# Cross attention scores as side by side 64-row matmuls of one head each, with a pair of maxima between their halves

## Chip, core and metric

The kernel runs on one core of a Trainium2 chip. The metric is the device time of one execution in microseconds (us), taken as the median of several runs. All times below come from runs of the kernel before and from one profiled execution of it.

## What is computed

Four layers run over a batch of B = 32 sequences of N = 100 tokens with H = 128 features and 16 heads of 8 features each. Three of them (L0, L1 and L3) are transformer layers: self attention, cross attention to a context of S = 1444 keys, and an MLP. L2 is a router layer. The change touches only the cross attention, which the three transformer layers have in this form:

```python
q = (norm(x) @ Wq).reshape(B, N, 16, 8).transpose(0, 2, 1, 3)
k = (ctx @ Wk).reshape(B, S, 16, 8).transpose(0, 2, 1, 3)      # S = 1444
v = (ctx @ Wv).reshape(B, S, 16, 8).transpose(0, 2, 1, 3)
w = softmax(einsum('bhqd,bhkd->bhqk', q, k) * 8 ** -0.5)
x = x + einsum('bhqk,bhkd->bhqd', w, v).reshape(B, N, 128) @ Wo + bo
```

## The kernel before

`cross_attention_phase` is one pipeline over the 32 batches. One pass of its body is called a slot here; slot t does the scores, exponentials and values of batch t, most row maxima of batch t + 1, the first maxima of batch t + 2, and preparation for batches t + 2 and t + 3. Each engine runs its own program in a fixed order, and semaphores tie them together.

The numbers stand as several bf16 parts. A head's keys and queries take 48 rows of a stack (`CROWS`, six products of parts by 8 features) and three more rows for the negated row maximum against rows of ones (`CROWS_NEG` = 51). `g.kst[s]` holds for each of 8 head pairs j the keys of head j in rows 0 to 50 and those of head j + 8 in rows 64 to 114. `g.qst[s]` has the queries: 200 columns per pair, where columns 0 to 99 are filled in the upper 64 rows and columns 100 to 199 in the lower 64, and the rest is zero. That zero fill is three memsets on POOL at the head of each cross phase (L1530), for which the SP queue waits.

A slot goes over 12 key tiles of 128 keys (the last has 36), called kt = 0 to 11. For each, PE (`pe_slot`) issues in this order:

- the scores (L1158, `pe_scores`): two halves of four matmuls, each over all 128 rows with 200 columns, so that one matmul gives the scores of both heads of a pair. Each half fills two PSUM banks, and waits until the exponential of the same half of the key tile before is done;
- a pair of maxima matmuls (L1137, `pe_max`): queries as weights, 482 or 480 keys as moving columns, the two heads of a pair in rows 0 to 47 and 64 to 111, in two PSUM banks;
- the values of the key tile before (L1175, `pe_values`): 32 matmuls with 9 weight columns and 100 moving columns, four side by side in 32-column groups;
- a second pair of maxima matmuls;
- at some key tiles a preparation step (`PREPS`): keys (L1114), values (L1120) or a transposition (L1106) of a coming batch. L0 and L1 have nine of them at five key tiles, L3 has six at six key tiles.

The maxima (48 per slot, called x = 0 to 47, four per key tile) and the preparation steps share a ring of three PSUM banks (`ring_tables`, `pe_ring_free`). A maxima matmul may start when what stood three places before it in the ring has been read: a maximum by DVE (L1294, `dve_max`, one reduction each), a preparation step by ACT. At two places the ring skips a bank. Besides the 48 reductions DVE copies the output of the batch before (L1323, once per slot after x = 2), folds the maxima (L1300) and makes the negated maxima (L1311 to L1318). In L0 it also takes statistics of a coming context (L1269, L1277). ACT does two exponentials per key tile (L1249) and reads the preparation steps. In its program, too, the order is fixed.

The code of the functions that the change touches, and of what calls them:

Of the kernel before, what the change touches and what calls it, by code (L numbers as in the profile page):

```python
# [5 lines left out]
BF16 = mybir.dt.bfloat16  # L6
# [978 lines left out]
def cross_attention_phase(g, wk, kb, wv, context):  # L985
# [16 lines left out]
    CUTS = [(0, S)] if normed else [(0, BANK), (BANK, 2 * BANK), (2 * BANK, S)]  # L1002
    ST_BANK, O_BANK, RING = 0, 4 * BANK, 5 * BANK
    TURN_KT = 8
    QHALF, KROWS = HALF, P
    K_RUNS = ((0, 3), (3, 2), (5, 1))
    KW = 16 * 2 * len(K_RUNS)
    Q_SLOTS = ((0, 3), (3, 2), (5, 1))
# [12 lines left out]
    with ExitStack() as st:  # L1021
# [30 lines left out]
        st_full, exp_done, pv_done = sem("scores_full"), sem("exp_done"), sem("pv_done")  # L1052
        o_read, o_moved = sem("o_read"), slots("o_moved")
        ones, zeros, ctx_std, stacks_set = sem("ones"), sem("zeros"), sem("ctx_std"), sem("stacks_set")
        ones_written, queries_zeroed, ctx_kept = sem("ones_written"), sem("queries_zeroed"), sem("ctx_kept")
        set_up = 1 + 2 * LAG


# [65 lines left out]
        def pe_max(slot, x):  # L1124

            k, t = max_tile(slot, x)
            if k is None:
                return
            s, r = k.s, k.r
            if t == 0:  # L1130
                wait(g.pe, k_loaded[s], 16 * (r + 1))
                wait(g.pe, qst_loaded[s], 16 * 12 * (r + 1))
            pe_ring_free(slot, x)
            at = bank_of(x)
            e, c, j = t % 2, (t // 2) % 3, t // 6
            a, w, row0 = starts[c], widths[c], HALF * e
            nc.tensor.matmul(ps[0:N, at:at + w], g.qst[s][row0:row0 + CROWS, j, N * e:N * e + N], g.kst[s][row0:row0 + CROWS, j, a:a + w],  # L1137
                             start=True, stop=True).then_inc(m_full, 1)

        def pe_turn_max(slot):  # L1140
# [8 lines left out]
        def pe_scores(k, n):  # L1149

            b, s, r = k.b, k.s, k.r
            kt, hf = n // 2, n % 2
            if n == 0:
                wait(g.pe, neg_loaded[s], 16 * 6 * (r + 1))
            wait(g.pe, exp_done, H2 * b + n - 1)
            for jj in range(4):
                o = ST_BANK + (2 * hf + jj // 2) * BANK + 2 * N * (jj % 2)
                ins = nc.tensor.matmul(ps[0:kts[kt], o:o + 2 * N], g.kst[s][0:KROWS, 4 * hf + jj, 128 * kt:128 * kt + kts[kt]],  # L1158
                                       g.qst[s][0:KROWS, 4 * hf + jj, :], start=True, stop=True)
            ins.then_inc(st_full, 1)  # L1160

        def pe_values(k, kt):


            b, s, r = k.b, k.s, k.r
            if kt == 0:
                wait(g.pe, o_read, b)
                wait(g.pe, p_read, S1 * b + PREP_INDEX["V2"] + 1)
            wait(g.pe, exp_done, H2 * b + 2 * kt + 2)
            for hf in range(2):  # L1170
                for e in range(2):
                    for jj in range(4):
                        h, q = 8 * e + 4 * hf + jj, 32 * jj
                        o = O_BANK + N * (2 * e + hf)
                        ins = nc.tensor.matmul(ps[q:q + VW, o:o + N], vals[s][:, kt, h, :],  # L1175
                                               probs[kt % 2][hf][:, N * (2 * jj + e):N * (2 * jj + e) + N],
                                               start=(kt == 0 and hf == 0 and e == 0), stop=(kt == KT - 1),
                                               skip_group_check=True)
            ins.then_inc(pv_done, 1)

        def pe_slot(slot):

            k, before = slot.k(0), slot.k(-1)
            for kt in range(KT):
                if k is not None:
                    pe_scores(k, 2 * kt)
                    pe_scores(k, 2 * kt + 1)
                pe_max(slot, 4 * kt)
                pe_max(slot, 4 * kt + 1)
                if kt == 0 and before is not None:  # L1190
                    pe_values(before, KT - 1)
                if kt and k is not None:
# [206 lines left out]
        def sp_stacks(k):  # L1399
# [7 lines left out]
            for e in range(2):  # L1407
                for part, (first, copies) in enumerate(Q_SLOTS):
                    src = g.qx[b // per, e, part].rearrange("(d j) n -> d j n", j=PAIRS)[:, :, N * (b % per):N * (b % per) + N]
                    for slot in range(first, first + copies):  # L1410
                        at = QHALF * e + HD * slot
                        sp.dma_start(g.qst[s][at:at + HD, :, N * e:N * e + N], src).then_inc(qst_loaded[s], 16)

        def sp_negmax(k):
            b, s, r = k.b, k.s, k.r
# [1 line left out]
            wait(sp, neg_steps, 4 * b + 4)  # L1417
            for e in range(2):
                for part in range(3):
                    at = QHALF * e + CROWS + part  # L1420
                    sp.dma_start(g.qst[s][at:at + 1, :, N * e:N * e + N], nparts[8 * e:8 * e + 8, part, :]).then_inc(neg_loaded[s], 16)

        def sp_keep_ctx(k):
            b, s, sp = k.b, k.s, g.sp
# [44 lines left out]
        with nc.Block() as block:  # L1469
# [56 lines left out]
            @block.gpsimd  # L1526
            def _(pool):
                g.pool = pool
                for s in range(LAG):
                    nc.gpsimd.memset(g.qst[s][:, :, :], 0.0).then_inc(queries_zeroed, 1)  # L1530
                if normed:
                    pool_norm(first)
                for b in range(-3, 1):
# [8 lines left out]
            def _(sp):  # L1542
# [3 lines left out]
                if normed:  # L1546
# [3 lines left out]
                            rows = slice(HALF * e + CROWS, HALF * e + HALF)  # L1550
                            sp.dma_start(g.kscr[s][rows, :], g.kst[0][rows, :, :].rearrange("p j n -> p (j n)")).then_inc(ones_written, 16)
                    sp.wait_ge(ones_written, 16 * 2 * LAG)
                sp.wait_ge(queries_zeroed, LAG)
                for b in range(-3, 1):
                    sp_slot(known(b))
                for i in range(loops):
# [407 lines left out]
def stack_scope(g, stack):  # L1964
# [1 line left out]
    nc = g.nc  # L1966
    g.serial += 1
    g.kst = [stack.enter_context(nc.sbuf_tensor(f"kst{s}_{g.serial}", [P, PAIRS, S], BF16)) for s in range(LAG)]
    g.qst = [stack.enter_context(nc.sbuf_tensor(f"qst{s}_{g.serial}", [P, PAIRS, 2 * N], BF16)) for s in range(LAG)]


def transformer_layer(g, a, pre, names, eps, l1):
# [166 lines left out]
```

## Time and profile before

| | us |
|---|---|
| median of 3 runs | 5788.03 |
| lowest and highest run | 5786.43, 5789.98 |
| span of the profiled execution, first to last instruction | 5784.8 |
| PE busy in it | 4939.3 (85%) |
| DVE busy in it | 3879.1 (67%) |
| ACT busy in it | 2941.4 (51%) |
| POOL busy in it | 1483.5 (26%) |
| maxima on DVE (L1294), busy | 2721.6 |
| scores on PE (L1158), busy | 999.1 |

The profiled execution was taken apart from the timed runs; its span is 3.2 us under their median, which is what lies around the first and the last instruction. In the page a group of instructions stands with its line, engine, result and inputs, shapes, count, then busy time, the mean ns of one, and the idle time of its engine just before them with what ended it. Matmuls are pipelined: the busy time of a run of them holds the tail of the last one, so the time from the start of one run to the start of the next says more of PE than the busy times do.

### The profile page before, as it was taken

To read this page: it belongs to the slowest core of one execution; us is meant where nothing else is said; L and a number is where in the kernel's file an instruction comes from. 1 tells how busy PE (TensorE), PEld (TensorE's weight loads), DVE (VectorE), ACT (ScalarE), POOL (GpSimd) and SP (SyncE) were. 2 spreads that over 40 slices of the span, in tenths; PEclk is the share of its full clock that TensorE was granted. 3 is DMA by queue.
4 is the path that set the end of the run, shared out by engine and by line. 5 is a ranking of instruction groups with operands and counts; after the bars stand their busy time and mean duration, and the time that the engine had idled before them with its cause. 6 is when DMAs were issued, how large, how long until landed. Compare 5 with 4: busy or idle time off the path is not lost. (4 is left out here: it accounts for less than half of the span.)

```text
span 5784.8 us, 149703 instructions
## 1 busy us (share of the span) xinstructions
PE 4939.3 (85%) x63218; PEld 3160.8 (55%) x63218; DVE 3879.1 (67%) x7814; ACT 2941.4 (51%) x4527; POOL 1483.5 (26%) x1198
## 2 busy tenths in 40 slices
PE   4858999999997676999999997888585899999998
PEld 2624555555564453666666663564363466666664
DVE  4537787888873554777777773555553788888883
ACT  2324666666664332666666663215322466666655
POOL 1024343443420104233332310000202333333320
PEclk7667999999998667999999998999766799999998
DMA  3334545545430425655565530540242555555540
GB/s 80 65 82 149 174 148 163 157 154 173 148 112 12 83 50 178 192 187 179 185 193 189 179 117 17 169 159 1 62 70 74 169 179 177 176 177 178 178 137 16
DMA packets 481593, 764.82 MB, mean 132 GB/s; under 512 B 144922, under 2 KB 381883, under 8 KB 468539
## 3 DMA queue, kind: packets, MB, share of 16 engines
q1 hardware_dynamic: 462394, 741.14, 43.1%
q10 hardware_dynamic: 18528, 14.11, 1.1%
q8 instruction: 499, 8.18, 0.6%
q14 instruction: 172, 1.40, 0.1%
HBM read 465.48 MB, written 287.75 MB: 130 GB/s over the span
## 5 line engine op out<-in xcount | busy, mean ns | idle before, releaser
L1294 DVE TENSOR_REDUCE maxima<-ps 100x1 f32<-100x482 f32 (+1 forms) x4608 | 2721.6, 650 | 829.4 <-PE ps L1137 822.6
L1249 ACT ACTIVATE probs<-ps 128x800 f32<-128x800 f32 (+1 forms) x2304 | 1799.8, 835 | 603.2 <-PE ps L1158 601.4
L1137 PE MATMUL ps<-kst,qst 48*100 48x482 bf16 (+1 forms) x4608 | 1101.4, 412 | 101.2 <-DMA qst<-cross_q_parts 49.3
L1346 POOL TENSOR_TENSOR kparts<-kf,zero 128x512 bf16<-128x512 f32 (+2 forms) x448 | 546.6, 1220 | 2103.5 <-ACT kf L1221 2064.2
L1175 PE MATMUL ps<-probs,vals 128*9 128x100 f32 x36864 | 1012.1, 250 | 5.5 <-ACT probs L1249 0.8
L1158 PE MATMUL ps<-qst,kst 128*128 128x200 bf16 (+1 forms) x9216 | 999.1, 250 | 10.3 <-DMA qst<-nparts 4.1
L1158 PEld LDWEIGHTS ps<-qst,kst 128*128 128x128 bf16 (+1 forms) x9216 | 761.4, 98 | 264.1 <-issue 152.8
L1175 PEld LDWEIGHTS ps<-probs,vals 128*9 128x9 f32 x36864 | 734.1, 90 | 255.1 <-issue 225.7
L1137 PEld LDWEIGHTS ps<-kst,qst 48*100 48x100 bf16 x4608 | 335.3, 119 | 616.6 <-DVE maxima L1294 325.9
L1227 ACT ACTIVATE vals<-ps 128x512 f32<-128x512 f32 (+1 forms) x288 | 162.1, 563 | 493.4 <-PE ps L1120 493.4
L1221 ACT ACTIVATE kf<-ps,perm_b_L 128x512 f32<-128x512 f32 (+1 forms) x288 | 190.5, 662 | 351.6 <-PE ps L1114 340.4
L1114 PE MATMUL ps<-ctxT,perm_wk_L 128*128 128x512 f32 (+1 forms) x576 | 305.6, 633 | 61.4 <-DVE maxima L1294 32.9
L763 ACT ACTIVATE probs<-ps 100x800 f32<-100x800 f32 x192 | 159.7, 837 | 366.5 <-PE ps L711 362.6
L1377 POOL TENSOR_TENSOR kparts<-kf,kparts 128x512 bf16<-128x512 f32 (+2 forms) x224 | 306.6, 1369 | 17.6
L1373 POOL TENSOR_TENSOR kf<-kf,kparts 128x512 f32<-128x512 f32 (+2 forms) x224 | 305.4, 1363 | 17.6
L775 DVE TENSOR_REDUCE maxima<-ps 100x4 f32<-100x400 f32 x384 | 205.6, 571 | 142.6 <-PE ps L689 141.8
L1120 PE MATMUL ps<-wkv_L,ctxT 128*128 128x128 f32 (+1 forms) x1536 | 227.8, 293 | 36.6 <-DVE maxima L1294 33.2
L689 PE MATMUL ps<-kst 96*100 96x100 bf16 x1152 | 143.9, 289 | 129.6 <-DMA kst<-k_parts 101.8
L1120 PEld LDWEIGHTS ps<-wkv_L,ctxT 128*128 128x128 f32 (+1 forms) x1536 | 184.3, 190 | 91.7 <-DVE maxima L1294 79.2
L689 PEld LDWEIGHTS ps<-kst 96*100 96x100 bf16 x1152 | 119.6, 193 | 154.8 <-issue 103.7
L1106 PE MATMUL ps<-ident,ctok 128*128 128x128 f32 (+1 forms) x768 | 131.2, 292 | 80.0 <-POOL ctok L1359 42.8
L1114 PEld LDWEIGHTS ps<-ctxT,perm_wk_L 128*128 128x128 f32 x576 | 95.3, 196 | 163.8 <-DVE maxima L1294 110.9
(261 smaller groups left out, 4528.8 us busy)
## 6 DMA issues: line engine op xcount, KB each, us to landing
kst<-ctx_k_stack SPq DMA_DIRECT2D x96, 2888.0 KB
ctx_k_stack<-kparts SPq DMA_DIRECT2D x192, 541.5 KB
ctx_k_stack<-kparts SPq DMA_DIRECT2D x192, 361.0 KB
ctok<-in_ctx_dram SPq DMA_DIRECT2D x64, 704.0 KB
ctx_k_stack<-kparts SPq DMA_DIRECT2D x192, 180.5 KB
ctx_turned<-ctxT SPq DMA_DIRECT2D x32, 722.0 KB, 3.3
cT<-ctx_turned SPq DMA_DIRECT2D x32, 722.0 KB, 5.5
ctxT<-ctx_turned SPq DMA_DIRECT2D x32, 722.0 KB
```

Of the source, the lines that this page charges most:

```text
L689: ins = nc.tensor.matmul(ps[0:N, o:o + N], queries[s][0:SROWS, h // 2, q0:q0 + N], keys[0:SROWS, h // 2, k0:k0 + N], start=True, stop=True)
L775: nc.vector.tensor_reduce(maxima[:, t // 4, c:c + 4], ps[0:N, at:at + CH].rearrange("p (h k) -> p h k", h=4), AX.X, ALU.max).then_inc(m_re ...
L1114: ins = nc.tensor.matmul(ps[:, at:at + w], wk, turned[s][:, a:a + w], start=True, stop=True)
L1120: ins = nc.tensor.matmul(ps[0:n, at + 128 * q:at + 128 * q + 128], turned[s][:, 128 * kt:128 * kt + n], wv, start=True, stop=True)
L1137: nc.tensor.matmul(ps[0:N, at:at + w], g.qst[s][row0:row0 + CROWS, j, N * e:N * e + N], g.kst[s][row0:row0 + CROWS, j, a:a + w], start=Tru ...
L1158: ins = nc.tensor.matmul(ps[0:kts[kt], o:o + 2 * N], g.kst[s][0:KROWS, 4 * hf + jj, 128 * kt:128 * kt + kts[kt]], g.qst[s][0:KROWS, 4 * hf ...
L1175: ins = nc.tensor.matmul(ps[q:q + VW, o:o + N], vals[s][:, kt, h, :], probs[kt % 2][hf][:, N * (2 * jj + e):N * (2 * jj + e) + N], start=( ...
L1249: nc.scalar.activation(probs[kt % 2][hf][0:kts[kt], :].rearrange("p (k n) -> p k n", k=2), src, ACT.Exp).then_inc(exp_done, 1)
L1294: nc.vector.reduce_max(maxima[:, col:col + 1], ps[0:N, at:at + widths[c]], AX.X).then_inc(m_read, 1)
L1346: return nc.gpsimd.tensor_tensor(out, src, g.zero[0:src.shape[0], 0:1].to_broadcast(list(src.shape)), ALU.add)
L1373: nc.gpsimd.tensor_tensor(kf[:, a:z], kf[:, a:z], parts[:, 0, a:z], ALU.subtract).then_inc(split, 1)
L1377: nc.gpsimd.tensor_tensor(parts[:, 2, a:z], kf[:, a:z], parts[:, 1, a:z], ALU.subtract).then_inc(parts_ready, 1)
```

## The change

The scores are cut into twice as many matmuls. Each has one head: 51 rows, at row 0 or at row 64, and 100 columns. The two heads of a pair follow each other and write into different PSUM banks of the half (bank e instead of bank jj // 2), and `pe_values` reads the probabilities in the new places. `g.qst` has 100 columns per pair instead of 200 and holds no zeros, so the memsets on POOL and the SP wait for them go, and the query and negated-maximum DMAs write to rows without a column offset. In `pe_slot` the second half of the scores now stands behind the first pair of maxima.

```diff
-            nc.tensor.matmul(ps[0:N, at:at + w], g.qst[s][row0:row0 + CROWS, j, N * e:N * e + N], g.kst[s][row0:row0 + CROWS, j, a:a + w],
+            nc.tensor.matmul(ps[0:N, at:at + w], g.qst[s][row0:row0 + CROWS, j, :], g.kst[s][row0:row0 + CROWS, j, a:a + w],
...
             for jj in range(4):
-                o = ST_BANK + (2 * hf + jj // 2) * BANK + 2 * N * (jj % 2)
-                ins = nc.tensor.matmul(ps[0:kts[kt], o:o + 2 * N], g.kst[s][0:KROWS, 4 * hf + jj, 128 * kt:128 * kt + kts[kt]],
-                                       g.qst[s][0:KROWS, 4 * hf + jj, :], start=True, stop=True)
+                for e in range(2):
+                    o = ST_BANK + (2 * hf + e) * BANK + N * jj
+                    rows = slice(HALF * e, HALF * e + CROWS_NEG)
+                    ins = nc.tensor.matmul(ps[0:kts[kt], o:o + N], g.kst[s][rows, 4 * hf + jj, 128 * kt:128 * kt + kts[kt]],
+                                           g.qst[s][rows, 4 * hf + jj, :], start=True, stop=True)
             ins.then_inc(st_full, 1)
...
-                                               probs[kt % 2][hf][:, N * (2 * jj + e):N * (2 * jj + e) + N],
+                                               probs[kt % 2][hf][:, N * (4 * e + jj):N * (4 * e + jj) + N],
...
                 if k is not None:
                     pe_scores(k, 2 * kt)
-                    pe_scores(k, 2 * kt + 1)
                 pe_max(slot, 4 * kt)
                 pe_max(slot, 4 * kt + 1)
+                if k is not None:
+                    pe_scores(k, 2 * kt + 1)
...
-                        at = QHALF * e + HD * slot
-                        sp.dma_start(g.qst[s][at:at + HD, :, N * e:N * e + N], src).then_inc(qst_loaded[s], 16)
+                        at = HALF * e + HD * slot
+                        sp.dma_start(g.qst[s][at:at + HD, :, :], src).then_inc(qst_loaded[s], 16)
...
-                for s in range(LAG):
-                    nc.gpsimd.memset(g.qst[s][:, :, :], 0.0).then_inc(queries_zeroed, 1)
...
-                sp.wait_ge(queries_zeroed, LAG)
...
-    g.qst = [stack.enter_context(nc.sbuf_tensor(f"qst{s}_{g.serial}", [P, PAIRS, 2 * N], BF16)) for s in range(LAG)]
+    g.qst = [stack.enter_context(nc.sbuf_tensor(f"qst{s}_{g.serial}", [P, PAIRS, N], BF16)) for s in range(LAG)]
```

PE's order before, in a looped slot of L3, from the end of key tile 5 to the start of key tile 7, with the key preparation L1114 at the end of key tile 6. L1158 is the scores, L1137 the maxima, L1175 the values:

```order
L1137 MATMUL ps<-kst1_419,qst1_419 100x482 x2
L1158 MATMUL ps<-qst0_419,kst0_419 128x200 x8
L1137 MATMUL ps<-kst1_419,qst1_419 100x480 x2
L1175 MATMUL ps<-probs10_509,vals0_509 9x100 x8
L1175 MATMUL ps<-probs11_509,vals0_509 9x100 x8
L1137 MATMUL ps<-kst1_419,qst1_419 100x482 x2
L1114 MATMUL ps<-ctxT0_509,perm_wk_L3 128x512
L1158 MATMUL ps<-qst0_419,kst0_419 128x200 x8
L1137 MATMUL ps<-kst1_419,qst1_419 100x482 x2
```

The same place in the changed kernel, where L1159 is the scores, L1136 the maxima, L1176 the values and L1113 the key preparation:

```order
L1136 MATMUL ps<-kst1_417,qst1_417 100x482 x2
L1159 MATMUL ps<-qst0_417,kst0_417 128x100 x8
L1136 MATMUL ps<-kst1_417,qst1_417 100x480 x2
L1159 MATMUL ps<-qst0_417,kst0_417 128x100 x8
L1176 MATMUL ps<-probs10_507,vals0_507 9x100 x8
L1176 MATMUL ps<-probs11_507,vals0_507 9x100 x8
L1136 MATMUL ps<-kst1_417,qst1_417 100x482 x2
L1113 MATMUL ps<-ctxT0_507,perm_wk_L3 128x512
L1159 MATMUL ps<-qst0_417,kst0_417 128x100 x8
L1136 MATMUL ps<-kst1_417,qst1_417 100x482 x2
```

Between a preparation step, or a second pair of maxima, and the next first pair there now stands half of the scores instead of all; between the first pair and the second there stand the other half and the values, where only the values stood. The program's count x8 holds 8 matmuls of 100 columns for a half, where it held 8 of 200 columns for both halves.

## Rows read from the trace of the kernel before

**Rows 1.** Page: parts 1 and 5 (busy, mean ns, idle before).
```profile
PE 4939.3 (85%) x63218; PEld 3160.8 (55%) x63218; DVE 3879.1 (67%) x7814; ACT 2941.4 (51%) x4527; POOL 1483.5 (26%) x1198
...
L1294 DVE TENSOR_REDUCE maxima<-ps 100x1 f32<-100x482 f32 (+1 forms) x4608 | 2721.6, 650 | 829.4 <-PE ps L1137 822.6
...
L1158 PEld LDWEIGHTS ps<-qst,kst 128*128 128x128 bf16 (+1 forms) x9216 | 761.4, 98 | 264.1 <-issue 152.8
```
**Rows 2.** Windows: L0's prologue, last slot, steady L3: PE, PEld, DVE, ACT, POOL, PEclk.
```profile
470.00:500.00 30.00, 26.18 (x59) 8.41 (x59) 22.48 (x55) 6.26 (x9) 16.77 (x8) 0.50 0.22 57
...
1734.00:1750.00 16.00, 15.73 (x367) 11.25 (x367) 0.00 (x0) 14.50 (x20) 0.00 (x0) 1.00 0.05 12
...
4700.00:5300.00 600.00, 567.48 (x9267) 371.15 (x9265) 491.76 (x899) 363.84 (x514) 212.75 (x204) 1.00 0.56 176
```
**Rows 3.** Timeline of DVE, one slot of L3: start, us, group, idle before.
```profile
5048.99 0.57 DVE L1323 COPY osb<-ps 128x400 f32<-128x400 f32 x1
```
**Rows 4.** The same timeline, further in that slot.
```profile
5050.76 2.37 DVE L1294 TENSOR_REDUCE maxima<-ps 100x1 f32<-100x482 f32 x4 [0.64 <-PE ps L1137]
...
5063.72 4.67 DVE L1294 TENSOR_REDUCE maxima<-ps 100x1 f32<-100x482 f32 x8 [1.10 <-PE ps L1137]
5069.45 2.37 DVE L1294 TENSOR_REDUCE maxima<-ps 100x1 f32<-100x482 f32 x4 [1.07 <-PE ps L1137]
...
5072.77 2.37 DVE L1294 TENSOR_REDUCE maxima<-ps 100x1 f32<-100x482 f32 x4 [0.70 <-PE ps L1137]
...
5076.07 6.92 DVE L1294 TENSOR_REDUCE maxima<-ps 100x1 f32<-100x480 f32 x12
5083.45 1.80 DVE L1294 TENSOR_REDUCE maxima<-ps 100x1 f32<-100x480 f32 x3 [0.45 <-PE ps L1137]
5085.17 0.56 DVE L1323 COPY osb<-ps 128x400 f32<-128x400 f32 x1
```
**Rows 5.** Timeline of PE in that slot, key tiles 6 and 7.
```profile
5066.72 0.41 PE L1137 MATMUL ps<-kst,qst 48*100 48x482 bf16 x2
5067.27 1.13 PE L1114 MATMUL ps<-ctxT,perm_wk_L 128*128 128x512 f32 x2 [0.15 <-DVE maxima L1294]
5068.23 0.85 PE L1158 MATMUL ps<-qst,kst 128*128 128x200 bf16 x8
5069.02 0.41 PE L1137 MATMUL ps<-kst,qst 48*100 48x482 bf16 x2
5069.35 0.88 PE L1175 MATMUL ps<-probs,vals 128*9 128x100 f32 x32
5070.16 0.41 PE L1137 MATMUL ps<-kst,qst 48*100 48x480 bf16 x2
```
**Rows 6.** Timeline of PE at the end of that slot.
```profile
5081.33 0.40 PE L1137 MATMUL ps<-kst,qst 48*100 48x482 bf16 x1
5081.89 0.40 PE L1137 MATMUL ps<-kst,qst 48*100 48x482 bf16 x1 [0.15 <-DVE maxima L1294]
5082.22 0.86 PE L1158 MATMUL ps<-qst,kst 128*128 128x200 bf16 x8
```
**Rows 7.** Timeline of PE in a self attention at the full clock.
```profile
228.77 0.54 PE L689 MATMUL ps<-kst,qextra 96*100 96x100 bf16 x8
```
**Rows 8.** Timeline of DVE in a slot of L1.
```profile
2863.80 2.37 DVE L1294 TENSOR_REDUCE maxima<-ps 100x1 f32<-100x482 f32 x4 [2.03 <-PE ps L1137]
```
**Rows 9.** Timeline of DVE in L0: statistics between maxima, and a slot's start.
```profile
1147.56 0.64 DVE L1294 TENSOR_REDUCE maxima<-ps 100x1 f32<-100x482 f32 x1
...
1148.32 0.64 DVE L1294 TENSOR_REDUCE maxima<-ps 100x1 f32<-100x480 f32 x1
...
1184.39 1.80 DVE L1294 TENSOR_REDUCE maxima<-ps 100x1 f32<-100x480 f32 x3 [0.82 <-PE ps L1137]
```
**Rows 10.** Timeline of POOL at the head of L1's cross phase.
```profile
2182.26 4.17 POOL L1530 MEMSET qst<- 128x1600 bf16 x3 [6.90 <-POOLq L264]
...
2193.32 1.04 POOL L1346 TENSOR_TENSOR kparts<-kf,zero 128x512 bf16<-128x512 f32 x1 [6.88 <-ACT kf L1221]
```

More of the change, by code:

```diff
@@ L1004, in cross_attention_phase @@
     TURN_KT = 8
-    QHALF, KROWS = HALF, P
     K_RUNS = ((0, 3), (3, 2), (5, 1))
@@ L1054, in cross_attention_phase @@
         ones, zeros, ctx_std, stacks_set = sem("ones"), sem("zeros"), sem("ctx_std"), sem("stacks_set")
-        ones_written, queries_zeroed, ctx_kept = sem("ones_written"), sem("queries_zeroed"), sem("ctx_kept")
+        ones_written, ctx_kept = sem("ones_written"), sem("ctx_kept")
         set_up = 1 + 2 * LAG
@@ L1419, in sp_negmax @@
                 for part in range(3):
-                    at = QHALF * e + CROWS + part
-                    sp.dma_start(g.qst[s][at:at + 1, :, N * e:N * e + N], nparts[8 * e:8 * e + 8, part, :]).then_inc(neg_loaded[s], 16)
+                    at = HALF * e + CROWS + part
+                    sp.dma_start(g.qst[s][at:at + 1, :, :], nparts[8 * e:8 * e + 8, part, :]).then_inc(neg_loaded[s], 16)
         def sp_keep_ctx(k):
```

## The prediction

> **What bounds the kernel now.** I read the page first. PE is busy for 85% of the span, DVE for 67%, and the group of 4608 maxima reductions on DVE (2721.6 us) stood idle for 829.4 us in front, nearly all of it until a maxima matmul of PE ended [rows 1]. So DVE is the engine with most of the necessary work in the cross phases, and PE is late for it at some places. To see which, I read one slot of L3 in the timeline of DVE. The slot is 36.18 us long, from one output copy at 5048.99 to the next at 5085.17 [rows 3, 4]. Where DVE is not made to wait, twelve reductions take 6.92 us, so one follows the other by (6.92 - 0.65) / 11 = 0.57 us and a key tile's four take 2.29 us [rows 4]. 48 of them make 27.5, and output copy, folding and negated maxima add some 1.7; what is left of 36.18 is seven waits of 0.45 to 1.33 us, together 6.4 us plus 0.08 each for the overlap that a wait breaks (five of the seven, the first and the last among them, stand in [rows 4]). Six of them follow a preparation step, the seventh (0.45) is the slot's start behind a skipped bank of the ring.
>
> Why such a wait is as long as it is, the timeline of PE shows. The preparation step (5067.27) starts when DVE has read a maximum two before the last; 0.96 us later the scores start, 0.79 after them the maxima pair (5069.02), and 0.43 after that DVE goes on (5069.45) [rows 4, 5]. The same chain in any key tile: a maxima matmul starts about 0.03 after the reduction three places before it ended, that is 0.68 after that one started (0.65 + 0.03); DVE takes its result 0.43 after its start [rows 4, 6].
>
> **What the change moves.** All sums are for one slot and then times the slots.
>
> *Length of the scores.* Eight matmuls of 200 columns take 0.79 us from the scores' start to the next maxima [rows 5], of which 8 x 200 / 2.4 GHz = 0.67 is columns. A half now is four side by side pairs of 100 columns. The nearest rows: eight matmuls of 100 columns with 100 weight columns, back to back at the full clock, take 0.54 us with the last one's tail of 0.21, so one follows the other by 0.047 us [rows 7]; and two maxima of 482 columns in the same two row halves take 0.41 together where one alone takes 0.40 [rows 5, 6], so the halves do run side by side. That gives 4 x 0.047 = 0.19 us for half of the scores. The far bound is 0.37, if the two of a pair ran one behind the other; I take 0.19, since the maxima use the very same rows.
>
> *Borders.* After a pair of maxima the scores or values follow 0.33 after it starts [rows 5, 6], although 482 columns at 2.4 GHz need 0.20: 0.13 is lost where the shape of the array changes. Between the preparation (full rows) and the scores (full rows) nothing is lost: 0.96 is its two passes. New scores and maxima have one shape, so I price the border between them at 0, at most 0.09 to 0.13; a new border of 0.10 comes up between preparation and scores.
>
> *Preparation steps, gain.* From the end of a preparation step to the next maxima there stood 0.79; now 0.10 + 0.19 = 0.29. The wait of DVE shrinks by 0.50 at each: 6 in L3 (1.07 to about 0.57), 5 in L0 and in L1, where the waits are longer still (2.03 [rows 8]). Gain 3.0 in L3, 2.5 in L1 and in L0. What is late next is the preparation itself, which does not change.
>
> *Start of a slot, gain.* The maxima pair comes 0.5 to 0.6 earlier, so the wait of 0.45 goes (0.5 with the overlap) in L3 and in L1. In L0 the 0.82 [rows 9] goes too, but there the second half of the scores waits for a late exponential and hands back some 0.35; I count 0.5 for each layer.
>
> *Second pair of maxima, loss.* The moved half stands between the first and the second pair, in front of the values. From the second matmul of the first pair to the second pair it was 0.33 + 0.81 = 1.14 (5069.02 to 5070.16) [rows 5]; now it is 0.20 columns + 0.19 scores + 0.13 border + 0.81 values = 1.33. That matmul may start 0.68 after the reduction three before it; the next pair's result is there 0.43 after its start. From reduction x to x + 4 this is 0.68 + 1.33 + 0.43 = 2.44 us, over the 2.29 that DVE needs; before, it was 2.25, just under. So each ordinary key tile now waits 0.14, and one behind a preparation step, where the pair starts together, 1.33 - 1.14 = 0.19. Key tile 9, behind the negated maxima, is spared, and in L0 those in which statistics stretch the pace to 0.76 (1147.56 to 1148.32) [rows 9]. Loss: L3 6 x 0.19 + 5 x 0.14 = 1.84; L1, where the output copy spares one more, 5 x 0.19 + 5 x 0.14 = 1.65; L0 3 x 0.19 + 2 x 0.14 = 0.85.
>
> *Net.* L3 3.0 + 0.5 - 1.84 = 1.7; L1 2.5 + 0.5 - 1.65 = 1.4; L0 2.5 + 0.5 - 0.85 = 2.1; together 5.2 us. Preparation runs up to three batches ahead, so 29 of 32 slots have it; at 28 whole ones this is 146 us. In the last slot of a layer only scores, values and exponentials run, PE for 15.73 and ACT for 14.50 of 16 us [rows 2]: PE's gain ends at ACT, at most 1.5 us of some 20, times 3: 4 us.
>
> *What costs nothing.* The POOL memsets (4.17 us per cross phase) end at 2186.4, and POOL's next work waits until 2193.32 for ACT [rows 10], so their removal gives 0 to a few us in all; I take 0. The SP queue keeps its order and its counts of DMAs. ACT and DVE keep their programs; ACT has 36% idle time in steady L3 (363.84 of 600 busy [rows 2]), and an exponential of the second half has a whole key tile until its values are due, so starting 0.4 later is covered by that.
>
> *Weights.* Twice as many loads are added, 9216 more with 98 ns each [rows 1]. In [rows 7] a load is as frequent as a matmul and still the step is 0.047, so they lie beside the matmuls; cost 0. The Trainium skill ("TensorE: Matmul & The Clock Gate", on packing small matmuls) says that weight loads overlap running matmuls only when the row group differs; by that, the loads of a row half would stand open in the new scores. The row just named shows loads of one row group hidden behind matmuls of the same, so here it doesn't hold as written.
>
> **Sum.** 5784.8 - 150 = 5635 for the profiled span, and 3 us lie around it: 5638 us against the median of 5788.03.
>
> **Rivals.**
> 1. *The second pair isn't late after all.* If a chain term is 0.15 shorter (the first score can slip into the free row half), the 4.3 us of loss per three slots vanish: 28 x 4.3 = 120 more, 5518. For it: the old chain had only 0.04 to spare and shows no wait. Against: nothing in the trace makes values shorter. 0.12.
> 2. *Borders remain.* If scores and maxima pay 0.09 and 0.13 in spite of one shape, preparation loses 16 x 0.09 and the second pairs 26 x 0.13, 4.8 of the 5.2: near 5773. Against: the free border between preparation and scores. 0.10.
> 3. *Slower: a pair runs one behind the other.* At 0.37 for a half each of 16 preparation steps and 26 second pairs is longer by 0.18: 7.6 lost against 5.2 won, 2.4 x 28 = 67, less the 4 of the last slots: 5851. It decides from 0.31 for a half (5.2 / 42 = 0.12 over 0.19). Against: the maxima of [rows 5]. 0.11.
> 4. *Slower: weight loads stand open.* With 0.098 in front of each pair a half takes 4 x (0.047 + 0.098) = 0.58, 0.39 more at each of 42 places: 16.4 - 5.2 = 11.2, x 28 = 313, 6100. 0.03.
> 5. *The clock falls.* In the prologue, where PE has only maxima and preparation, it was granted 0.50 with PE called busy for 26.18 of 30 us; in steady slots and the last slot it is 1.00, the latter without maxima [rows 2]. The change leaves PE fewer rows and columns to do. At half clock in the slots a key tile's PE work (about 1.7) would double to 3.4 against 2.3: over 1000 us, or 100 for a tenth of the time. Against: values stay whole. 0.04.
> The changed kernel not doing what it says is no case of its own: the halves and the order stand in the code as told.
>
> **How the numbers follow.** The forecast has 0.60: 5638, by itself 5590 to 5690. The range reaches over rivals 1 and 2, 5510 to 5790, and so holds 0.82. Less than 0.2% (12 us) is about what a measurement here can't tell from no change. Faster: forecast, rival 1 and over half of rival 2, 0.78; same 0.04; slower 0.18.
>
> **What would show it.** Scores halves of about 0.19 from start to the next matmul and 0.20 from a maxima pair to the half behind it (right), or 0.33 (rival 2), 0.37 (3), 0.58 (4). DVE's waits behind preparation steps 0.5 shorter, none at a slot's start, and new waits of 0.1 to 0.2 in front of each second pair; none of these is rival 1. Slots of about 34.5 in L3, 37.0 in L1, 38.3 in L0. A granted clock under 1.00 in steady slots would be rival 5. The prediction is wrong if a half is over 0.31, or if ACT becomes the late one.

## The result, and the profile after

The changed kernel took 5636.99 us (median of 4 runs, 5632.6 to 5668.36), the kernel before on the same chip 5787.23 (4 runs, 5784.2 to 5789.98). The ratio is 0.9755, with a 95% interval of 0.9731 to 0.978: faster by 2.4%, 1 us beside the forecast of 5638. The profiled execution has a span of 5637.8 us, 147.0 less than before.

The page of the changed kernel (parts 1 and 5: busy time, share and count; then group, busy, mean ns of one, idle before and its releaser). The reductions are now L1296, the maxima matmuls L1136, the scores L1159:

```profile
PE 4728.2 (84%) x72434; PEld 3027.6 (54%) x72434; DVE 3931.6 (70%) x7814; ACT 2981.4 (53%) x4527; POOL 1466.6 (26%) x1189
...
L1296 DVE TENSOR_REDUCE maxima<-ps 100x1 f32<-100x482 f32 (+1 forms) x4608 | 2771.2, 649 | 636.3 <-PE ps L1136 577.9
...
L1159 PE MATMUL ps<-qst,kst 51*128 51x100 bf16 x18432 | 988.1, 209 | 15.9 <-ACT probs L1251 9.8
L1159 PEld LDWEIGHTS ps<-qst,kst 51*128 51x128 bf16 x18432 | 713.2, 100 | 366.1 <-issue 128.0
```

DVE's idle time in front of the maxima fell from 829.4 us [rows 1] to 636.3. That is 193 us, more than the kernel won. Some of it came back as busy time: 2771.2 against 2721.6 us, since each new wait breaks the overlap of two reductions.

The timeline of PE in a slot of L3, key tiles 4 to 6 (start, us, group, idle before), which answers to [rows 5]:

```profile
4858.81 0.35 PE L1159 MATMUL ps<-qst,kst 51*128 51x100 bf16 x8
4859.01 0.37 PE L1136 MATMUL ps<-kst,qst 48*100 48x482 bf16 x2
4859.21 0.34 PE L1159 MATMUL ps<-qst,kst 51*128 51x100 bf16 x8
4859.49 0.87 PE L1176 MATMUL ps<-probs,vals 128*9 128x100 f32 x32
4860.29 0.41 PE L1136 MATMUL ps<-kst,qst 48*100 48x480 bf16 x2
4860.69 1.12 PE L1113 MATMUL ps<-ctxT,perm_wk_L 128*128 128x512 f32 x2
4861.75 0.35 PE L1159 MATMUL ps<-qst,kst 51*128 51x100 bf16 x8
4861.94 0.47 PE L1136 MATMUL ps<-kst,qst 48*100 48x482 bf16 x2
```

A half takes 0.19 to 0.20 us (4858.81 to 4859.01, 4861.75 to 4861.94). From the pair of maxima to the half behind it are 0.20, just the columns. From the preparation step (4860.69) to the scores are 1.06, that is 0.96 and a border of 0.10. From the half to the values are 0.28: 0.19 and a border of 0.09.

DVE in the same slot, from one output copy to the next, for [rows 3, 4]:

```profile
4849.21 0.57 DVE L1325 COPY osb<-ps 128x400 f32<-128x400 f32 x1
4849.69 1.80 DVE L1296 TENSOR_REDUCE maxima<-ps 100x1 f32<-100x482 f32 x3
4852.16 1.22 DVE L1296 TENSOR_REDUCE maxima<-ps 100x1 f32<-100x480 f32 x2 [0.66 <-PE ps L1136]
4853.74 1.22 DVE L1296 TENSOR_REDUCE maxima<-ps 100x1 f32<-100x482 f32 x2 [0.36 <-PE ps L1136]
4855.20 3.70 DVE L1296 TENSOR_REDUCE maxima<-ps 100x1 f32<-100x482 f32 x6 [0.23 <-PE ps L1136]
4859.41 2.54 DVE L1296 TENSOR_REDUCE maxima<-ps 100x1 f32<-100x482 f32 x4 [0.51 <-PE ps L1136]
4862.34 1.23 DVE L1296 TENSOR_REDUCE maxima<-ps 100x1 f32<-100x482 f32 x2 [0.39 <-PE ps L1136]
4863.77 3.70 DVE L1296 TENSOR_REDUCE maxima<-ps 100x1 f32<-100x482 f32 x6 [0.20 <-PE ps L1136]
4867.83 1.23 DVE L1296 TENSOR_REDUCE maxima<-ps 100x1 f32<-100x482 f32 x2 [0.37 <-PE ps L1136]
...
4883.70 0.56 DVE L1325 COPY osb<-ps 128x400 f32<-128x400 f32 x1
```

The slot is 34.49 us long, against 36.18. Of the six waits behind preparation, the four that were 1.07 to 1.33 are now 0.36 to 0.51, and the last went from 0.70 to 0.10. The first is as long as before (0.64, now 0.66 at 4852.16), but stands one pair later. The wait of 0.45 at the slot's start is gone. New are waits of 0.10 to 0.25 in front of second pairs (4855.20 and 4863.77, for example).

Where the 147 us came from, by the starts of the output copies in both traces. A whole slot at the full clock went from 40.35 to 37.58 us in L0, from 38.41 to 36.29 in L1 and from 36.19 to 34.48 in L3. The 27 intervals between the copies that answer to whole slots gave 72.8, 34.9 and 44.7 us, together 152.4. The first slots of the layers, from the first scores to the first copy, gave 8.0 (2.6, 3.0 and 2.5). The last four slots of the layers, 28 to 31, took 23.7 us longer than before: slot 28 gained 4.9 in all three layers together and slot 31 gained 4.4, but slots 29 and 30 lost 33.0. The rest, 10.2, lies outside these slots; 7.3 of it stands ahead of L0's first scores, where programs that are the same up to there repeat only to some 7 us (first score at 487.24 here, at 492.29 and 485.39 in the runs with repeated scores in the last and in the whole slots).

Most of the loss in the last slots, and L1's small share, go with one thing, the clock. Windows of the changed kernel (us, then PE, PEld, DVE, ACT and POOL busy, PEclk, DMA share, GB/s): a steady piece of L3 and of L0, then 58 us of L0's slots 29 and 30, a piece of L3's slot 30, a piece of L1, and L1's slots 29 and 30 whole:

```profile
4744.00:4778.00 34.00, 31.86 (x637) 20.30 (x626) 29.48 (x53) 21.65 (x31) 12.47 (x12) 1.00 0.57 181
1540.00:1575.00 35.00, 31.97 (x642) 20.70 (x632) 28.98 (x66) 25.66 (x36) 14.83 (x9) 1.00 0.52 163
1601.50:1659.50 58.00, 52.13 (x770) 32.32 (x770) 35.98 (x64) 24.36 (x30) 0.00 (x0) 0.50 0.03 9
5472.20:5502.90 30.70, 28.99 (x428) 18.25 (x426) 17.75 (x33) 12.96 (x16) 0.00 (x0) 0.50 0.03 10
2461.60:2482.10 20.50, 20.27 (x269) 12.99 (x270) 13.79 (x27) 8.26 (x10) 2.53 (x3) 0.50 0.64 186
3292.10:3357.70 65.60, 51.62 (x1249) 35.28 (x1251) 49.15 (x90) 40.32 (x52) 0.00 (x0) 0.99 0.23 76
```

In steady slots 1.00 (2.4 GHz) was granted, in most of slots 29 and 30 of L0 and of slot 30 of L3 0.50 (1.2 GHz). L0's slots 29 and 30 took 45.4 and 39.3 us where they had taken 35.1 and 28.7; L3's slot 30 took 38.9 instead of 28.7. In L1 short falls lengthened many whole slots from 36.3 to 37.3, and one of 20.5 us to 41.2: its 27 intervals sum to 1002.2, where 27 x 36.29 is 979.8. So the clock cost 22 us there, and about 28 in the last slots by the run that held it (below). In L1 itself slots 29 and 30 took 65.7 us at 0.99, in L0 84.7, with 1249 matmuls in either. The kernel before had none of this: no granted clock under 1.00 stands in its cross slots.

### The profile page after: what moved, and what is told of

Read it like the earlier page. It is cut to its first block and busy times, and to the rows that moved or that the text cites. A ratio compares the mean times of both kernels' runs of the same rounds, so it can differ in the third digit from the quotient of the medians.

```text
span 5637.8 us, 168125 instructions
## 1 busy us (share of the span) xinstructions
PE 4728.2 (84%) x72434; PEld 3027.6 (54%) x72434; DVE 3931.6 (70%) x7814; ACT 2981.4 (53%) x4527; POOL 1466.6 (26%) x1189
## 5 line engine op out<-in xcount | busy, mean ns | idle before, releaser
L1296 DVE TENSOR_REDUCE maxima<-ps 100x1 f32<-100x482 f32 (+1 forms) x4608 | 2771.2, 649 | 636.3 <-PE ps L1136 577.9
L1251 ACT ACTIVATE probs<-ps 128x800 f32<-128x800 f32 (+1 forms) x2304 | 1843.3, 835 | 600.1 <-PE ps L1159 593.7
L1136 PE MATMUL ps<-kst,qst 48*100 48x482 bf16 (+1 forms) x4608 | 1299.8, 413 | 229.4 <-DVE maxima L1296 164.9
L1176 PE MATMUL ps<-probs,vals 128*9 128x100 f32 x36864 | 1043.9, 255 | 1.2 <-ACT probs L1251 0.9
L1159 PE MATMUL ps<-qst,kst 51*128 51x100 bf16 x18432 | 988.1, 209 | 15.9 <-ACT probs L1251 9.8
L1159 PEld LDWEIGHTS ps<-qst,kst 51*128 51x128 bf16 x18432 | 713.2, 100 | 366.1 <-issue 128.0
L1136 PEld LDWEIGHTS ps<-kst,qst 48*100 48x100 bf16 x4608 | 421.3, 122 | 727.9 <-DVE maxima L1296 449.7
L1176 PEld LDWEIGHTS ps<-probs,vals 128*9 128x9 f32 x36864 | 754.4, 92 | 103.4 <-issue 2.3
L1113 PE MATMUL ps<-ctxT,perm_wk_L 128*128 128x512 f32 (+1 forms) x576 | 304.0, 631 | 28.8 <-DMA ctxT<-ctx_turned 17.5
L1119 PE MATMUL ps<-wkv_L,ctxT 128*128 128x128 f32 (+1 forms) x1536 | 227.5, 292 | 17.7 <-DVE maxima L1296 15.4
L1119 PEld LDWEIGHTS ps<-wkv_L,ctxT 128*128 128x128 f32 (+1 forms) x1536 | 184.3, 190 | 68.8 <-DVE maxima L1296 49.7
L220 POOL TENSOR_TENSOR sq<-sq,parts 128x400 f32<-128x400 f32 x36 | 34.0, 943 | 542.5 <-ACT parts L209 542.5
```

The lines of the kernel that those rows point to most:

```text
L1113: ins = nc.tensor.matmul(ps[:, at:at + w], wk, turned[s][:, a:a + w], start=True, stop=True)
L1119: ins = nc.tensor.matmul(ps[0:n, at + 128 * q:at + 128 * q + 128], turned[s][:, 128 * kt:128 * kt + n], wv, start=True, stop=True)
L1159: ins = nc.tensor.matmul(ps[0:kts[kt], o:o + N], g.kst[s][rows, 4 * hf + jj, 128 * kt:128 * kt + kts[kt]], g.qst[s][rows, 4 * hf + jj, :], ...
L1251: nc.scalar.activation(probs[kt % 2][hf][0:kts[kt], :].rearrange("p (k n) -> p k n", k=2), src, ACT.Exp).then_inc(exp_done, 1)
L1296: nc.vector.reduce_max(maxima[:, col:col + 1], ps[0:N, at:at + widths[c]], AX.X).then_inc(m_read, 1)
```

## The experiments

**The order undone.** One edit in `pe_slot` puts both halves of the new scores ahead of the first pair again.

```diff
                 if k is not None:
                     pe_scores(k, 2 * kt)
+                    pe_scores(k, 2 * kt + 1)
                 pe_max(slot, 4 * kt)
                 pe_max(slot, 4 * kt + 1)
-                if k is not None:
-                    pe_scores(k, 2 * kt + 1)
```

> The changed kernel with its order undone: both 64-row halves of the scores stand before the first pair of maxima again. My theory (the 64-row pairs win 0.50 us at each preparation step, the order alone costs 0.14 to 0.19 us at each second pair of maxima, and the moved half is what stands there): against the changed kernel each preparation step is 0.19 us longer (6, 5, 5 per slot in L3, L1, L0) and the waits of the second pairs (1.84, 1.65, 0.85 us per slot) go, so 1.3 us less over three slots and 28 x 1.3 = 36 us less: about 5600 us. Rival, the order is what helps (it hides the second half behind the maxima): the preparation steps are 0.19 us longer and nothing is won, 28 x 16 x 0.19 = 85 us more, about 5720. Rival, the order does not matter: 5637 within 10.

Measured: 5597.54 us (5593.72 to 5606.26), ratio to before 0.9674 (0.966 to 0.9689). This is faster than the change as made, and near the 5600 expected. The timeline of PE in L3 shows both halves in 0.37 to 0.38 us, then the pair and the values without a half between them (the scores are L1159, the values L1176 here too):

```profile
4706.27 0.53 PE L1159 MATMUL ps<-qst,kst 51*128 51x100 bf16 x16
4706.64 0.37 PE L1136 MATMUL ps<-kst,qst 48*100 48x482 bf16 x2
4706.94 0.87 PE L1176 MATMUL ps<-probs,vals 128*9 128x100 f32 x32
4707.74 0.42 PE L1136 MATMUL ps<-kst,qst 48*100 48x480 bf16 x2
```

From pair to pair are 1.10 us, 0.18 less than the 1.28 of the changed kernel (4859.01 to 4860.29). Undisturbed slots take 37.83 in L0, 35.91 in L1 and 33.4 in L3, against 37.58, 36.29 and 34.48. So with the new scores the order wins 0.25 in L0 and loses 0.38 and 1.08 in L1 and L3, 1.21 in all where the expectation had 1.3: what it takes from the way of a preparation step it puts in the way of the next second pair, and there are 12 second pairs in a slot against five or six preparation steps and a start. In L3 many of this kernel's slots are longer than 33.4 (median 33.89), most of them with the clock at 1.00. In the longest, 36.3 us, PE waits for a transfer, that of the negated maxima, and the clock is 0.50 for 3.4 us from 5265.4 on, so both have a part in it:

```profile
5265.57 0.85 PE L1159 MATMUL ps<-qst,kst 51*128 51x100 bf16 x16 [1.31 <-DMA qst<-nparts]
```

DVE in a slot of L1 of this kernel, at the first and the last pair of maxima that wait behind preparation; in the kernel before, the first of them was 2.03 [rows 8]:

```profile
2764.85 2.37 DVE L1295 TENSOR_REDUCE maxima<-ps 100x1 f32<-100x482 f32 x4 [1.68 <-PE ps L1136]
...
2778.82 4.65 DVE L1295 TENSOR_REDUCE maxima<-ps 100x1 f32<-100x480 f32 x8 [1.45 <-PE ps L1136]
```

**The order alone.** The kernel before, with its 128-row scores, zero fill and memsets, and the same move of the second half behind the first pair.

```diff
                 if k is not None:
                     pe_scores(k, 2 * kt)
-                    pe_scores(k, 2 * kt + 1)
                 pe_max(slot, 4 * kt)
                 pe_max(slot, 4 * kt + 1)
+                if k is not None:
+                    pe_scores(k, 2 * kt + 1)
```

> The kernel before with the new order alone: 128-row scores of 200 columns, the second half behind the first pair of maxima. My theory: a half is 0.35 us long and pays borders, so a preparation step wins 0.35, but a second pair of maxima comes 1.59 instead of 1.14 us after the first, and a key tile's chain is 0.68 + 1.59 + 0.43 = 2.70 against 2.29 us of DVE: 0.41 to 0.45 us lost at each of 26 second pairs of three slots, in all 4.4 us more per three slots, times 28 = 123: about 5910 us, slower than before. Rival, the order is what helps: under 5787, down to 5700.

Measured: 5882.7 us (5880.93 to 5888.89), ratio 1.0167 (1.0152 to 1.0182), slower by 1.7%, as expected in kind (5910). Slots take 40.38 in L0 (as before), 39.6 in L1 (1.2 more) and 37.77 in L3 (1.6 more). PE and then DVE in L3 (scores L1158, maxima matmuls L1137, reductions L1295):

```profile
4860.87 0.52 PE L1158 MATMUL ps<-qst,kst 128*128 128x200 bf16 x4
4861.32 0.41 PE L1137 MATMUL ps<-kst,qst 48*100 48x482 bf16 x2
4861.66 0.52 PE L1158 MATMUL ps<-qst,kst 128*128 128x200 bf16 x4
4862.10 0.88 PE L1175 MATMUL ps<-probs,vals 128*9 128x100 f32 x32
4862.91 0.41 PE L1137 MATMUL ps<-kst,qst 48*100 48x480 bf16 x2
```
```profile
4861.76 1.23 DVE L1295 TENSOR_REDUCE maxima<-ps 100x1 f32<-100x482 f32 x2 [0.77 <-PE ps L1137]
4863.35 1.22 DVE L1295 TENSOR_REDUCE maxima<-ps 100x1 f32<-100x480 f32 x2 [0.37 <-PE ps L1137]
```

From pair to pair are 1.59 us, so each second pair is late by some 0.37. Both borders that the change removes stand here: 0.34 from pair to half (0.20 are columns) and 0.45 from half to maxima (0.33 are columns). The order taken alone is a loss (some 96 us against the kernel before); the win of the change comes from the shape of the scores, which alone, in the kernel with the order undone, wins 189.

**Which of two heads first.** The changed kernel with the loops over heads and pairs exchanged, so that four matmuls of the upper rows stand ahead of four of the lower rows.

```diff
-            for jj in range(4):
-                for e in range(2):
+            for e in range(2):
+                for jj in range(4):
```

> The changed kernel with the two loops of the scores exchanged: four matmuls of the upper rows, then four of the lower rows, so that only the border between the two fours can run side by side. Same matmuls, weights, banks and count. My theory (the pairs run side by side): a half takes about 7 x 0.047 = 0.33 us instead of 0.19, 0.14 more at each of 16 preparation steps and 26 second pairs of three slots, 5.9 x 28 = 165 us more: about 5800. Rival (the gain is from columns without zeros, from the missing border, or from the issue rate, not from running side by side): a half stays at 0.19 and the time at 5637.

Measured: 5663.65 us (5659.48 to 5678.88), ratio 0.9795 (0.9779 to 0.9811). The expectation of 5800 missed by far: a half doesn't become longer.

```profile
4770.14 0.36 PE L1159 MATMUL ps<-qst,kst 51*128 51x100 bf16 x8
4770.34 0.50 PE L1136 MATMUL ps<-kst,qst 48*100 48x482 bf16 x2
```

It takes 0.20 as before, and in the records the eight still start two by two, 12 to 13 ns apart (4770.144 and .157, .199 and .211, .247 and .260, .290 and .303), although matmuls of different row halves are now four places apart in the program. The records don't name the rows; that the two of a pair are of different halves follows from the next run, where matmuls of one half start 0.042 to 0.055 apart. Steady slots at the full clock are as long as the changed kernel's (37.6, 36.3, 34.5). What it loses is 27 us, 20 between the two profiles; these 20 stand in L0, where some slots take 38.6 to 40.8 us with the clock at 0.50 for a part of them.

**All in one row half.** The changed kernel with every score matmul in rows 0 to 50; the second head's scores are not computed, its place gets the first head's.

```diff
-                    rows = slice(HALF * e, HALF * e + CROWS_NEG)
+                    rows = slice(0, CROWS_NEG)
```

> The changed kernel with all score matmuls in the upper 64 rows: the same number, columns, banks and order, but the second head of a pair is given the keys and queries of the first, so its scores are not computed. Nothing can run side by side then. My theory (running side by side is what makes a half short): a half takes 8 x 0.047 = 0.37 us instead of 0.19, 0.18 more at each of 16 preparation steps and at the 14 second pairs behind them in three slots; at the other second pairs the scores can run beside the late maximum of the lower rows, which gives the 0.18 back. 30 x 0.18 x 28 = 151 us more: about 5790. Rival (a half is short for its 51 rows, its 100 columns without zeros or its issue rate): a half stays at 0.19 and the time at 5637.

Measured: 5993.86 us (5969.91 to 6049.33), ratio 1.0379 (1.0325 to 1.0434).

```profile
4855.10 0.53 PE L1159 MATMUL ps<-qst,kst 51*128 51x100 bf16 x8
4855.47 0.51 PE L1136 MATMUL ps<-kst,qst 48*100 48x482 bf16 x2
4855.67 0.52 PE L1159 MATMUL ps<-qst,kst 51*128 51x100 bf16 x8
```

The half takes 0.37 where it took 0.19 to 0.20. The same count of the same matmuls and loads takes twice as long when they share their rows: the halves of the changed kernel do run side by side. Before, half of the scores took 0.79 / 2 = 0.39 [rows 5], so columns without zeros and a row count of 51 give hardly anything by themselves. The mechanism came as expected and the total didn't: L3's slots at the full clock grew by 1.0 to 35.5, but L0's took 38.8 to 45.5 us and L1's 37.8 to 45.3, with falls of the clock over 20 us long, and L0's last slots ran at 0.50 for 126 us.

**More work for PE in the last slots.** In the changed kernel the first half of the scores is issued three times over (same result, same place) in slots 29 and 30. These have scores, values and maxima, but no preparation of keys any more; slot 29 still has the three value steps (L1119) of the last batch, slot 30 has no preparation and only a part of the 48 maxima.

```diff
-            for jj in range(4):
+            for jj in [jj for _ in range(times) for jj in range(4)]:
...
-                    pe_scores(k, 2 * kt)
+                    pe_scores(k, 2 * kt, 3 if slot.k(3) is None and slot.k(1) is not None else 1)
```

> The changed kernel, where in slots 29 and 30 of each layer (behind the last preparation steps) the first half of the scores is issued three times in place of once, with the same result: 0.38 us more PE work per key tile, in front of the first pair of maxima where PE has 0.7 us to spare. Only the clock can gain by it. In the trace of the changed kernel these slots of L0 took 45.4 and 39.3 us at a granted clock of 0.50, against 35.1 and 28.7 at 1.00 before; in L3 slot 30 took 38.9 against 28.7. My theory (PE has too little to do there since the change, so the clock falls): the clock stays at 1.00 in them, and 10 + 10 + 10 us come back, about 5606 in an execution like the profiled one. Rival (these slots are longer through a wait of the new order, and the clock fell because of the waits): they stay as long or are longer, 5637 or more.

Measured: 5625.37 us (5611.95 to 5631.79), ratio 0.9717 (0.9703 to 0.9732). Windows in L0's last slots:

```profile
1600.00:1620.00 20.00, 18.02 (x509) 12.84 (x497) 18.18 (x35) 11.82 (x15) 0.00 (x0) 1.00 0.23 79
1620.00:1640.00 20.00, 16.57 (x468) 11.97 (x460) 16.73 (x29) 11.12 (x15) 0.00 (x0) 1.00 0.06 17
```

With more matmuls issued the clock stayed at 1.00 there, and L0's slots went from 45.4 and 39.3 to 36.0 and 30.4, L3's slot 30 from 38.9 to 29.6: 27.6 us. So the long last slots were mostly the clock's doing, and more work for PE held it. Over all profiles this stands out in slot 30: with the repeated scores (here and in the three runs below) the clock was 1.00 in it in all 12 cases, and in the three kernels without them (the changed one, the order undone, the heads in turn) between 0.59 and 0.73 in 7 of 9. The amount of work alone doesn't decide it, since L0 and L1 of the changed kernel have the same matmuls there. The run itself won 12 us of the 28 (22 by the ratios). In its profile L1 had fewer but longer falls than the changed kernel's (12 with 102.4 us in all, three of them 20.5 long, against 18 with 78.3 and one of 20.5), where the two programs are the same.

**The same in the whole slots.** The filling also in all key tiles but the first with no preparation step in front of them, once for the changed kernel and once for the one with the order undone.

```diff
-                    pe_scores(k, 2 * kt)
+                    pe_scores(k, 2 * kt, 3 if slot.k(1) is not None and kt and (slot.k(3) is None or kt - 1 not in PREPS) else 1)
```

> The changed kernel, where the first half of the scores is issued three times in place of once, with the same result, in each key tile but the first that has no preparation step in front of it (six in a slot of L0 and L1, five in L3, and all but the first in slots 29 and 30). 0.38 us more PE work in each, in front of the first pair where PE can spare it. Theory of the clock (PE has too little to do in stretches without preparation): no granted clock under 1.00 from the first whole slot to the last, slots of L1 all at 36.3 us instead of 36.3 to 41.2, slots 29 and 30 under 36 and 30: 15 to 30 us from L1 and 31 from the last slots, about 5585. Rival (the clock falls for the waits, or the added work makes the first pair late): 5637 or more.

Measured: 5605.88 us (5602.42 to 5609.76), ratio 0.9697 (0.9681 to 0.9713), some 33 us under the changed kernel by the ratios (25 by the medians, each against its own runs of before), and 21 over the 5585 expected. In L0's last slots:

```profile
1580.00:1640.00 60.00, 52.55 (x1418) 38.21 (x1410) 50.05 (x91) 34.90 (x45) 0.00 (x0) 1.00 0.29 93
```

Most slots at the full clock stay at 37.6, 36.3 and 34.5, so the repeated matmuls are free in them; some 24 of the 81 whole slots are 0.2 to 0.9 us longer at 1.00, 11 us together, and why stays open. In all three cross phases four short falls are left, and L1's 31 intervals sum to 1108.9 instead of 1124.3, L0's to 1138.3 instead of 1156.4.

> Both halves of the scores before the first pair, as in e1, with the same repeated half as in e7. The trace of e1 has slots of 37.8, 35.9 and 33.4 us at the full clock, and longer ones where the clock falls or negated maxima land late. Theory: without the falls of the clock 37.8, 35.9 and 33.4 hold in nearly all slots and the last slots are under 36 and 30: 25 to 35 us under e1's 5597, about 5567, the fastest of all. Rival: PE's added work makes the first pair late, and it is 5600 or more.

Measured: 5636.73 us (5629.79 to 5641.92), ratio 0.9747 (0.9733 to 0.9762): a miss by 70 us, slower than without the filling. Slots of L0 take 38.2 where PE is at the full clock (0.4 more), and in most of them the clock falls, which makes them 38.7 to 40.9. One such fall (windows ahead of it, in it, behind it):

```profile
640.00:643.70 3.70, 3.02 (x59) 1.50 (x52) 3.70 (x8) 3.66 (x5) 0.83 (x1) 1.00 0.54 114
643.70:647.10 3.40, 3.19 (x56) 2.15 (x58) 1.61 (x4) 1.60 (x3) 3.32 (x3) 0.50 0.94 204
647.10:650.50 3.40, 2.96 (x66) 2.01 (x63) 3.40 (x8) 1.57 (x2) 1.64 (x2) 1.00 0.87 261
```

Ahead of it PE has waits of 0.16 for DVE and of 0.16 and 0.28 for ACT's exponentials. So it isn't enough to give PE more to do: with this order the added work goes along with more falls in L0, not fewer. Why is open.

**The order undone, filled in the last slots alone.**

Its edits are that of the order undone and that of the last slots, together.

> The kernel of e1_both_halves_first, with the first half of the scores issued three times over (same weights, same columns, same place in PSUM) in slots 29 and 30 alone, where no maxima matmuls run any more; the whole slots stay as in e1. In e1's profile the clock was 0.50 for 17.1 us in L0's last whole slots and for 20.5 us in L1's, and slot 30 took 33.8 (L0) and 35.1 us (L1); where this filling stood already (e5) the same slots took 28.3 and 29.3. Theory, that the clock falls there because PE has too little to do: 33.8 to 28.3, 35.1 to 29.3 and L3's last slot from 20.6 to 18.5, 13 us in all, 5584 us, the shortest of all kernels run. Rival, that the falls only move into the whole slots around (as e5's stood in L0's whole slots): the tail is shorter and the sum is not, 5597 or above.

The expectation is wrong in one thing: maxima do run in slots 29 and 30; what has ended is the preparation of keys, and in slot 30 that of values. Measured: 5593.78 us (5581.34 to 5604.7, 5 runs), ratio 0.9676 (0.9662 to 0.969). Slot 30 took 28.3 us in all three layers, as the theory had it, and no granted clock under 1.00 stands in slots 29 to 31 of L0 and L1. But the ratio is that of the kernel without the filling (0.9674): what slots 29 to 31 give, 15 us between the two profiles, is less than the runs differ (23 us). The two are the fastest kernels run, about 0.8% under the change, and these runs can't tell one from the other.

## Why the prediction came out right

**The length of a half** was right: 0.19 to 0.20, and for the reason given. One row half takes 0.37, which is the far bound of the prediction, so rival 3 is out. The weight loads cost nothing (rival 4): 18432 loads of 100 ns each stand in the page of after, and the half holds no time for them.

**The borders** were right: 0 between scores and maxima, 0.10 between preparation and scores; rival 2 is out. Ahead of the values 0.13 was counted and 0.09 came. The trace shows a loss where the shape changes and none where it stays, as the Trainium skill says ("TensorEngine Tiling (Array Packing)", Key Properties: a change of tiling mode drains TensorE).

**Preparation steps and slot starts** were priced too low. Taken wait by wait in one slot of each layer, DVE's waits behind preparation and at the slot's start shrank by 4.03 us in L0, 3.91 in L1 and 4.03 in L3, where 3.0, 3.0 and 3.5 stood in the sum. L0's first two show 0.53 and 0.52, near the 0.50 of the sum (1.45 to 0.92), and so does L1's first (2.03 to 1.51); most others show 0.7 to 0.8 (L1: 1.83 to 1.12, 1.38 to 0.64, 1.10 to 0.39). The step that failed is the sum's reading of waits one by one: DVE now waits already at the second pair, and so much less is left to wait for at the preparation step behind it. The kernel with the order undone, in which no second pair waits in the slots read of L0 and L1, bears it out: there four of the five steps shrank by 0.34 or 0.35 (L1: 2.03 to 1.68, 1.83 to 1.48, 1.10 to 0.76, 1.80 to 1.45), which is 0.53 less the second half's 0.19, and no longer 0.7. The fifth shrank by 0.56, and why it differs stays open.

**The second pair of maxima** is late, as the chain of 2.44 us against 2.29 said; rival 1 is out. The first scores do slip in beside a late maximum, as that rival had it, but the other four stand behind it, and from the second matmul of a first pair to the second pair the slot of L3 shows 1.32 at ten of twelve key tiles, where 1.33 was said. It costs more than was counted: new waits and broken overlaps take 2.35 us in L3 (1.84 in the sum), 1.80 in L1 (1.65) and 1.28 in L0 (0.85). In the sum the new waits were counted without the overlap that each breaks (0.65 us of busy time more in the L3 slot). In L3 the two errors cancel (1.69 came, 1.7 was said); in L0 and L1 the gain is larger than said (2.77 and 2.1 against 2.1 and 1.4).

**The clock** (rival 5) was given 0.04 and came in part. [rows 2] showed 1.00 for the last slot, which has no maxima, and for steady slots, which have maxima and all of the preparation. Slots 29 and 30, which have maxima and little or no preparation, weren't read, and it is there that it fell to 0.50 for long; in L1 it fell in whole slots too. At 2.1 and 1.4 for L0 and L1 the sum was 40 us short; the clock took about 50 in the last slots and L1. So the total of 5638 is right by luck, by two errors that offset each other, and the forecast of the mechanism is better borne out by the slots than by the total. By an estimate from the slots, at full clock throughout the change would give some 50 us more, near 5587, just under the lower end of the forecast's own range; the run nearest to that, with whole slots filled, took 5605.88.

**The last slot** of a layer won 4.4 us over the three layers, as the 4 of the sum had it. **Slots 29 and 30** stood at nothing in it, without a reason given, and lost 33.0: 27.6 of that came back in three of these slots where the clock was held, and the rest goes with the order (35.0 and 28.3 us in L0 with the order undone and filled, 36.0 and 30.4 with the new order and filled, 35.1 and 28.7 before). The first slots and what lies outside, 8.0 and 10.2, stood in the sum at nothing too. **The memsets** gave nothing, as said: from L0's last output copy to L1's first maxima matmul, the stretch in which they stood, are 477.2 us before and 477.3 after.

What isn't settled: which part of the time ahead of L0's scores (7.3 us) is the change's, and what sets the short falls of the clock in L0 and L1, which differ between programs that are alike in those slots.

## What to carry to other kernels

Here matmuls of 48 and 51 rows, in pairs on the two row halves, cost the columns of one (0.19 us against 0.37), with no border between the two kinds; price each shape change in the order (about 0.1 here) and look for orders with fewer of them. Moving work away from in front of a late producer puts it in front of another: the chain of the next one, with its slack of a few hundredths here, has to be worked out before the move, and in L1 and L3 it was the worse place. When work is taken from PE, read the granted clock of every stage afterwards, the short stages at the end of a phase too.

## What the runs showed of the hardware

- Two row halves take their matmuls apart from each other. With four of one half ahead of four of the other in the program they still ran two by two, and the half took 0.20 us. In the changed kernel, where the second matmul of a first pair had to wait for DVE, it started at 4870.556; four scores started from 4870.562 on, 0.044 to 0.055 apart, beside it, and the other four from 4870.800 on. By their spacing the first four are those of the free half. The Trainium skill says that matmuls keep the program's order in start and end ("TensorE: Matmul & The Clock Gate", Part 3, The mechanism). Within one row half nothing here speaks against it; across the halves the runs differ from it.
- The clock was 0.50 over 58.00 us in which PE was called busy for 52.13, and 1.00 over steady pieces with a like share (31.86 of 34). The busy time of a trace, which holds the tails of pipelined matmuls, does not tell whether the clock will hold. Three times the matmuls of one half in the same slots held it (18.02 of 20 busy, 1.00).
- The falls are not fixed by the program of the slots in which they stand: L1's whole slots, the same in the changed kernel and in the one with only the last slots filled, had 18 falls with 78.3 us in one profile and 12 with 102.4 in the other.
